# A graph network's prologue rebuilt: blocks ranked ahead of the count, a centred sum of squares, keys and values ahead of the degrees

## The reference, cut to what matters

```python
h = jnp.maximum(_layernorm(x, axis=-1), 0.0)          # input norm, then ReLU
x = x + _L0_gnn_ref(h, edge_index, ...)
# inside, for each of L = 2 layers:
xn = _layernorm(x, ln1_g[l], ln1_b[l])
deg = segment_sum(ones, src); deg = (deg - deg.mean()) / (std(deg, ddof=1) + 1e-6)
pos = xn @ Wpos[l] + bpos[l] + deg[:, None] * Wdeg[l][0] + bdeg[l]
xp = xn + pos
q, k, v = xp @ Wq[l] + bq[l], xp @ Wk[l] + bk[l], xp @ Wv[l] + bv[l]
att = einsum('ehd,ehd->eh', q[dst], k[src]) / scale    # then clip, segment softmax over dst
x = x + (segment_sum(v[src] * alpha, dst) @ Wo[l] + bo[l])
x = x + (gelu(layernorm(x) @ W1[l] + b1[l]) @ W2[l] + b2[l])
```

## Time and profile before

| | us |
|---|---|
| median of 3 runs | 2203.33 (2202.92 to 2208.78) |
| the profiled execution's own time | 2208.83 |
| its span | 2207.1 |
| busy in the span: PE / DVE / ACT / POOL | 1423.0 / 1714.1 / 934.4 / 1578.9 |
| GpSimd's gathers L765, x1612 | 1528.0 busy, 948 ns each |

### The profile page before, as it was taken

The page is one execution under the profiler, slowest core; times in us unless marked ns, Lnnn a source line. Parts: engine busy times, 40 slices in busy tenths (PEclk is TensorE's granted clock), DMA queues, the critical chain, the costliest instruction groups (busy, mean ns, idle before and its releaser), DMA issues.

```text
span 2207.1 us, 32470 instructions
## 1 busy us (share of the span) xinstructions
PE 1423.0 (64%) x8220; PEld 1249.0 (57%) x8220; DVE 1714.1 (78%) x5109; ACT 934.4 (42%) x2172; POOL 1578.9 (72%) x1669
## 2 busy tenths in 40 slices
PE   4765566666767666666666556566575756666666
PEld 3655555555556555655556555555565655555555
DVE  7849878878878878887866777777777778777775
ACT  7424353533535353534453334344353435343343
POOL 6377777777777777777726777777777777777773
PEclk9769888877888887777877878877778778777787
DMA  3355444444444444454424444444444444444441
GB/s 99 100 160 166 141 134 148 130 143 134 136 140 130 149 134 142 131 148 134 137 60 126 135 134 129 134 134 138 134 129 134 138 135 128 135 134 138 125 138 52
DMA packets 123506, 289.30 MB, mean 131 GB/s; under 512 B 31525, under 2 KB 57057, under 8 KB 123329
## 3 DMA queue, kind: packets, MB, share of 16 engines
q0 software_dynamic: 77824, 212.31, 33.5%
q1 hardware_dynamic: 45504, 74.92, 10.4%
HBM read 275.44 MB, written 8.38 MB: 129 GB/s over the span
## 4 chain that ended last, share of the span: by engine, by line
POOL 54%; issue 21%; DVE 8%; PE 8%; DMA 4%; ACT 4%; SPq 1%; DVEq 1%; ACTq 0%; POOLq 0%
POOL kvr L765 52%; DMA kvr<-kv_table,srcidx 4%; PE bank L1005 3%; PE bank L1018 2%; DVE agg L1561 2%; POOL q L726 1%; DVE kvr L1217 1%; ACT apart L1172 1%; DVE prod L1534 1%; ACT onehotT L1176 1%; DVE msg L1552 1%; ACT L1134 1%; PE bank L961 1%; ACT L1181 1%; DVE onehot L1527 1%
## 5 line engine op out<-in xcount | busy, mean ns | idle before, releaser
L765 POOL DMA_INDIRECT kvr<-kv_table,srcidx x1612 | 1528.0, 948 | 560.6 <-issue 480.1
L1005 PE MATMUL bank<-q,onehotT 128*128 x3328 | 610.6, 341 | 717.6 <-DVE prod L1534 455.0
L1005 PEld LDWEIGHTS bank<-q,onehotT 128*128 128x128 f32 x3328 | 518.5, 238 | 821.8 <-issue 821.5
L1018 PE MATMUL bank<-msg,onehot 128*128 128x136 f32 x3328 | 613.9, 344 | 4.1 <-DVE msg L1552 4.0
L1181 ACT ACTIVATE bank<-attc 128x32 f32<-128x32 f32 x404 | 81.2, 201 | 1190.3 <-DVE attc L1547 1189.8
L1018 PEld LDWEIGHTS bank<-msg,onehot 128*128 128x128 f32 x3328 | 575.2, 253 | 5.4 <-DVE msg L1552 5.2
L1534 DVE TENSOR_TENSOR prod<-kvr,bank 128x512 f32<-128x512 f32 x404 | 276.5, 684 | 295.8 <-DMA kvr<-kv_table,srcidx 260.9
L1561 DVE TENSOR_TENSOR agg<-agg,bank 128x136 f32 x1628 | 470.6, 289 | 42.5 <-PE bank L1018 36.5
L1172 ACT ACTIVATE apart<-relT,minus_p 128x512 bf16<-128x512 bf16 x416 | 293.8, 706 | 0.5
L1527 DVE TENSOR_TENSOR onehot<-bank,rel 128x512 f32<-128x512 f32 x416 | 282.6, 682 | 0.4
L1552 DVE TENSOR_TENSOR msg<-kvr,bank 128x512 f32<-128x512 f32 x404 | 274.5, 679 | 7.9 <-ACT bank L1181 7.9
(11 more groups left out here) (205 smaller groups left out, 861.1 us busy)
## 6 DMA issues: line engine op xcount, KB each, us to landing
relT<-rel_table SPq DMA_DIRECT2D x104, 512.0 KB, 4.2
kvr<-kv_table,srcidx POOLq DMA_INDIRECT x1612, 2.8
qkv<-kv_table SPq DMA_DIRECT2D x25, 128.0 KB, 3.4
kv_table<-qkv SPq DMA_DIRECT2D x25, 128.0 KB, 3.1
kv_table<-kvr SPq DMA_DIRECT2D x12, 256.0 KB, 2.1
w<-weights SPq DMA_DIRECT2D x2, 840.0 KB, 7.5
loops<-x_in SPq DMA_DIRECT2D x5, 320.0 KB, 5.4
x<-x_nat SPq DMA_DIRECT2D x25, 64.0 KB, 1.8
```

The lines of the kernel that those rows point to most:

```text
L765: pool.indirect_dma_start(kvr[:, n % RING, j, :], None, kv_table[l], bass.IndirectOffsetOnAxis(ap=srcidx[:, step:step + 1], axis=0)).then_ ...
L1005: mm = pe.matmul(bank[2][:, j * D:(j + 1) * D], onehotT[:, m % OHT, j, :], q[:, bass.ds(ranks[j + h], 1), :].rearrange("p a c -> p (a c)") ...
L1018: mm = pe.matmul(sum_ps(n, k), onehot[:, m % OH, j, :], msg[:, n % 2, j, :], start=(m, j) == of[0], stop=(m, j) == of[-1])
```

## The change

- `rank_blocks` stands ahead of the first count step, `place_steps` between the first and the second.
- The input's squares are taken first, as squares of (first element - x), then the plain sums; DVE corrects the variance by the square of (mean - first element). The squares no longer wait for the mean.
- Layer 1's norm is cut in two halves (12 and 13 blocks), each with its own ReLU, squares, root and normalising pass, interleaved on ACT; DVE's small steps for them stand between the low and the high instruction of a count step.
- The transposes and the first two pairs of keys and values move in between the count steps 10 to 13 on PE. The first four pairs (`KV_EARLY`) are copied out of PSUM with `kv_bias` added before the degrees are known (`keep_early`); `add_degrees` then adds `deg * u` in one instruction per block. For the nine other pairs the bias comes from a three-row matmul on PE (`bias_row`), and the one DVE instruction per block reads PSUM. The order of the pairs is 0, 4, 1, 5, 2, 6, 3, 7, 8 to 12.
- The rows of edge numbers are transposed after the degree sum and before pair 10; layer 2's `u` and fold move behind the queries, the degree's transpose and reordering into the queries, the one-hots of the loop's steps 0 and 1 between query groups 3 and 4.
- SP's 25 copies of the rectified input stand behind the 25 of the queries, ahead of the third `rel_rows`.

```diff
+KV_EARLY = 4
+KV_ORDER = [k for i in range(KV_EARLY) for k in (i, KV_EARLY + i)] + list(range(2 * KV_EARLY, len(KV_PAIRS)))
+HALVES = [(0, 12), (12, BLOCKS)]
...
# SP
-            sp.wait_ge(s_relu, BLOCKS)
-            for b0, nb in NAT:
-                for j, r in enumerate(read_block_ranks(ENG.SP, b0, nb)):
-                    sp.dma_start(x[:, bass.ds(r, 1), :], x_nat[:, b0 + j:b0 + j + 1, :]).then_inc(s_x_ranked, 16)
...
                     sp.dma_start(q[:, bass.ds(r, 1), :], q_nat[:, c % 2, j:j + 1, :]).then_inc(s_q_ranked[c % 2], 16)
+            sp.wait_ge(s_relu, BLOCKS)
+            for b0, nb in NAT:
...
# PE
                 for j in range(nb):
                     o = use(0, i, "kv")[:, j * KV:(j + 1) * KV]
-                    mm = pe.matmul(o, xnT_nat[...], w[0][:, W_QKV + D:W_QKV + 3 * D], start=True, stop=True)
+                    mm = pe.matmul(o, xnT_nat[...], w[0][:, W_QKV + D:W_QKV + 3 * D], start=True, stop=i < KV_EARLY)
+                    if i >= KV_EARLY:
+                        mm = bias_row(o, 0, R_QKV + 1, 2)
...
+                elif k == 10:
+                    turn_nat(0)
+                    turn_nat(1)
+                elif k == 11:
+                    turn_nat(2)
+                    keys_values(0)
+                elif k == 12:
                     turn_bias()
+                    turn_nat(3)
+                    keys_values(1)
+                elif k == 13:
+                    turn_nat(4)
+                    turn_nat(5)
+                    turn_nat(6)
+                elif k == 14:
+                    spread_bias()
...
# ACT
+            rectify(*HALVES[0])
+            square(*HALVES[0])
...
+            first_layer_root(0)
+            rectify(middle, BLOCKS)
+            square(*HALVES[1])
+            first_layer_norm(0)
+            first_layer_root(1)
+            for c in range(3):
+                untranspose_nat(c)
+            act.wait_ge(*read(0, 2, "T"))
+            first_layer_norm(1)
...
# DVE
+            def add_degrees(i):
+                b0, nb = KV_PAIRS[i]
+                k = TURN[0, i, "kv"][0]
+                to = kv_of(b0, nb)
+                if i < KV_EARLY:
+                    dve.wait_ge(*read(0, i, "kv"))
+                else:
+                    dve.wait_ge(*full(0, i, "kv"))
+                for j in range(nb):
+                    of = to[:, j, :] if i < KV_EARLY else bank[k][:, j * KV:(j + 1) * KV]
+                    ins = dve.scalar_tensor_tensor(out=to[:, j, :], in0=u_deg[:, 0, D:3 * D], scalar=deg[:, 0, b0 + j:b0 + j + 1], in1=of, op0=ALU.mult, op1=ALU.add)
```

More of the change, by code:

```diff
@@ L723, in _ @@
             pool.wait_ge(s_tileno, 1)
[L724 to L735, removed]
+            fetch_rows(step_dst, dst_tiles)
+            fetch_rows(step_src, src_tiles)
+            split_bias()
             pool.wait_ge(s_rows, 16 * 2 * SC)
@@ L849, in keys_values @@
                 b0, nb = KV_PAIRS[i]
+                if i == 0:
+                    pe.wait_ge(*read(0, 0, "fold"))
+                pe.wait_ge(*read(0, (b0 + nb - 1) // 4, "T"))
                 claim(0, i, "kv")
@@ L894, in _ @@
+            keys_values(2)
             pe.wait_ge(s_counts, 1)
@@ L1052, in _ @@
                     act.wait_ge(s_x[b // X_BLOCKS], 16)
+                if b == 0:
+                    act.wait_ge(s_digits, 2)
+                act.activation(xn_nat[:, b, :], x_raw[:, b, :], ACT.Square, bias=x_raw[:, b, 0:1], scale=-1.0, accum_out=x_sums[:, 1, b:b + 1]).then_inc(s_squares_in, 1)
+            for b in range(BLOCKS):
                 act.activation(x_nat[:, b, :], x_raw[:, b, :], ACT.Identity, accum_out=x_sums[:, 0, b:b + 1]).then_inc(s_sums_in, 1)
-            act.wait_ge(s_mean_in, 1)
@@ L1055, in _ @@
-            for b in range(BLOCKS):
-                act.activation(x_nat[:, b, :], x_raw[:, b, :], ACT.Square, bias=shift[:, b:b + 1], accum_out=x_sums[:, 1, b:b + 1]).then_inc(s_sums_in, 1)
             root_var(s_var_in, 1, mv[:, :, 1], std[:], s_std)
-            act.wait_ge(s_shift, 1)
-            for b in range(BLOCKS):
-                act.activation(x_nat[:, b, :], x_raw[:, b, :], ACT.Relu, bias=shift[:, b:b + 1], scale=rstd[:, b:b + 1], accum_out=x_sums[:, 0, b:b + 1]).then_inc(s_relu, 1)
@@ L1072, in _ @@
-            root_var(s_var0, 1, mv[:, :, 1], std[:], s_std)
-            act.wait_ge(s_shift, 2)
-            act.wait_ge(s_squares, BLOCKS)
-            for b in range(BLOCKS):
-                act.activation(xn_nat[:, b, :], x_nat[:, b, :], ACT.Identity, bias=shift[:, b:b + 1], scale=rstd[:, b:b + 1]).then_inc(s_xn_nat, 1)
-            act.wait_ge(*full(0, 0, "biasT"))
-            act.copy(bias_parts[:], bank[TURN[0, 0, "biasT"][0]][0:PARTS * L * RC, 0:D]).then_inc(read(0, 0, "biasT")[0], 1)
@@ L1080, in _, with rectify, square @@
-            for c in range(NATS):
+            def rectify(b0, b1):
+                for b in range(b0, b1):
+                    act.activation(x_nat[:, b, :], x_raw[:, b, :], ACT.Relu, bias=shift[:, b:b + 1], scale=rstd[:, b:b + 1], accum_out=x_sums[:, 0, b:b + 1]).then_inc(s_relu, 1)
+            def square(b0, b1):
+                act.wait_ge(s_relu, b1)
+                act.wait_ge(s_squares_in, BLOCKS)
+                for b in range(b0, b1):
+                    act.activation(xn_nat[:, b, :], x_nat[:, b, :], ACT.Square, accum_out=x_sums[:, 1, b:b + 1]).then_inc(s_squares, 1)
@@ new lines, in first_layer_root, with first_layer_norm @@
+            def first_layer_root(h):
+                b0, b1 = HALVES[h]
+                root_var(s_var0, h + 1, mv[:, b0:b1, 1], std[:, b0:b1], s_std)
+            def first_layer_norm(h):
+                b0, b1 = HALVES[h]
+                act.wait_ge(s_shift, h + 2)
+                act.wait_ge(s_squares, b1)
+                for b in range(b0, b1):
+                    act.activation(xn_nat[:, b, :], x_nat[:, b, :], ACT.Identity, bias=shift[:, b:b + 1], scale=rstd[:, b:b + 1]).then_inc(s_xn_nat, 1)
@@ L1187, in _ @@
             edge_spread(1)
+            for l in range(1, L):
+                keep_degree(l)
             for l in range(L):
@@ L1348, in _ @@
+            dve.wait_ge(*read(0, 0, "wide"))
+            keep_early(0)
+            keep_early(1)
             dve.wait_ge(s_hist_mm, HSTEPS)
```

302 lines of the change are left out of this document (171 added, 131 removed).

## The result

The changed kernel takes 2200.52 us in the median (2197.87 to 2206.04, 12 runs), the kernel before 2205.26 on the same chip (2202.92 to 2209.64, 12 runs). The ratio is 0.9979, 95% interval [0.997, 0.9988]: 4.7 us faster, 2.6 to 6.6 by the interval. Forecast were 11.9 us. The profiled execution took 2200.12 us, its span 2198.4. It is 8.7 us shorter than the profiled execution before (2208.83), which was one of the slower ones of its kernel: the traces, one execution each, show more of the gain than the medians do.

A forecast was written before the change was run, and what follows sets the result against it. The loop runs at GpSimd's gather pace, so the first gather's start and the messages' lead decide. The smaller of 13.9 and 9.7 + 2.2, 11.9 us, off the 2203.33 median gives about 2191.5 us; range 2186 to 2206.

The forecast's parts named there:

- The rule: Loop start: the kernel gains the smaller of G and A + 2.2, forecast 11.9 us.
- ring: Messages ahead of the loop's gathers: least slack of the first steps 2.2 us, at the 45th gather, needing step 3's message.
- G: How much earlier GpSimd's first gather starts: 13.9 us, at 97.0 instead of 110.9.
- A: How much earlier the loop's first product on DVE comes: 9.7 us, at 128.3 instead of 137.96.
- I take nothing, with 0 and 3 us as bounds: SP: third rel_rows queued behind the 25 copies of x leaves some 12 us after the first product, just in time.
- some 4 us: Time for the third rel_rows load to land, wanted by ACT about 16 us after the first product.
- The second term: Prologue to GpSimd's first gather: count steps, then pairs bound by PE, put it at 97.0.
- the count ends after 76: Sign that the forecast is wrong; DVE's count was laid out to end at 72.5, against 81.2 before.
- DVE's row: DVE up to the count's end: 6.4 + 2.5 us of waits gone, 1 new, about 1 for the start.
- Rival 1: PE's clock falls in the pairs of keys and values: gain 2.6, time 2200.7; chance 0.2.
- Rival 2: GpSimd is kept out for several count steps, more than once: 2208.5 with three such waits, 2220 with four; chance 0.09.
- Rival 3: Queries hold the loop back, first product only 3 us earlier: gain 5.2, time 2198; chance 0.09.

The follow-up runs named there:

- experiment 3: Changed kernel with SP's 25 copies of x back in their old place, ahead of the count's end: 2196.04 us, ratio 0.9954 to the kernel before.
- experiment 4: Changed kernel with only the third rel_rows load issued ahead of the 25 copies of x: 2197.36 us, ratio 0.9957 to the kernel before.
- its repetition: Changed kernel, unchanged, measured and profiled once more: 2200.53 us, ratio 0.9974 to the kernel before.
- Experiment 8: experiment 3's kernel with three of GpSimd's four operations on 128x896 given to ACT: 2194.94 us, ratio 0.9948 to the kernel before.
- experiment 6: Changed kernel, third rel_rows load behind 12 of 25 copies, or behind 25 plus 12 more; first on a slow chip, rerun: 2198.82 and 2207.64 us.

## Why the prediction was wrong

**The rule held, within some 2 us.** First gather and ring decide. The prediction's rule, the smaller of G and A + 2.2, gives 8.6 us for experiment 3 with its own first gather and first product (102.3 and 130.4), 7.7 for experiment 4 (103.2 and 131.8). Measured are 10.1 (7.5 to 13.0) and 9.5 (6.0 to 12.8).

**The step that failed is SP's: "I take nothing, with 0 and 3 us as bounds".** Putting the 25 copies of x ahead of the third `rel_rows` cost 0.0021 of the ratio, 4.6 us: the mean of after and its repetition (0.99765) against that of experiments 3 and 4 (0.99555). By the widths of the four intervals this is an estimate of 2 to 7 us. Two things in the step were wrong.

The first is the time to land. The forecast had the load leave 12 us behind the first product, land in "some 4 us" and be wanted at 16. It left at 11.4, was wanted at 14.8 (146.16 - 3.10) and had landed at 17.9. So landing took 6.5 us. The trace of the kernel before shows it for this one load, in a window around its issue (size in KB, median us from issue to landing):

```profile
relT<-rel_table SPq DMA_DIRECT2D x1, 512.0 KB, 6.4
```

The second is what the delay falls on. The forecast charged it to step 4's message, which leads its gather by 3 us. But step 3's message stands behind step 4's product on DVE, and it has the least lead of all, 2.2 us, of which 0.3 pass between a message's end and the gather that it frees (156.15 and 156.43). It came 2.0 us later against the first product; with 1.9 us of lead, and 0.1 by which the first gather gained more than the first product (9.8 and 9.7), that makes the 0.2 us in the trace. So the chain of waits is shown, but this execution lost 0.2 us by it, not 4.6.

**The second term off is the first gather.** 101.1 instead of 97.0. The count ends 3.7 us late, PE starts the first pair with bias 2.2 late (81.61 instead of 79.4), and 8.5 pairs of 1.70 instead of 1.5 are 1.7 more. The prediction named "the count ends after 76" as a sign against itself, and it ended at 76.2. By the rule min(G, A + 2.2) this turns 11.9 into min(9.8, 9.7 + 2.2) = 9.8. So 11.9 - 2.1 for the gather - 4.6 for SP's load = 5.2 us, and the mean of both runs of after gives 0.00235 x 2205 = 5.2. That the two agree to a tenth is luck: the 4.6 is a difference of the same ratios, and each of them is uncertain by 2 us or more.

**DVE's row.** The waits of 6.4 and 2.5 us went, as forecast. In their place came 0.9 more than laid out at `position_bias`, and 2.45 + 0.73 between 45.93 and 54.35, where GpSimd's operations on 128x896 lie, 4.1 in all, against a count that ends 3.7 late. Experiment 8 shows that GpSimd's operations cause the second part. The page "SBUF — State Buffer" of the Trainium skill, section "SBUF: two separate sides", says that a DVE instruction with two inputs in SBUF and a GpSimd instruction that reads SBUF contend for a lock, which goes to whoever starts first for the whole instruction. I had weighed only that GpSimd comes late; this trace agrees for the other direction as well, DVE being late by 2.45 us.

**Rivals.** Rival 1 (the clock falls in the pairs): false, 1.00 from 79 to 98 us. Rival 2 (GpSimd is kept out over several count steps): false, no fetch took over 2.5 us and GpSimd was done with the last of this work by 54.3. Rival 3 (the queries hold the loop back): false, the first product came 9.7 us earlier as forecast, though its time (2198) is near the measured one. PE's queries ran at 2.4 GHz for the greater part (0.93 from 98 to 115), where I had priced 1.2 GHz; SP's copies, 19.8 us as before, set the first product all the same.

**What stays open.** Where the 4.6 us of the medians go. The profiled executions show 0.2 and 0.5 us of them as a late 45th gather in the kernel after, and where the load left behind 12 copies they show none, while its time is 3 us above that of the load first. Nor do they show the rest elsewhere: from the first gather to the end of the span are 2097.3 and 2093.9 us in the two profiles of after, 2094.3 and 2098.4 in those of experiments 3 and 4, and much of that spread is the wait for layer 2's table (42.3 to 48.2 us over the profiles, those on the slow chip of experiment 6 left aside). Either the lateness differs from one execution to the next and the profile caught mild ones, or a part of it is the copies' traffic after all. The intervals, 2 to 3.5 us to each side, don't tell these apart. Beyond the threshold the price is clear, in trace and time: 8 us later cost 10 us at the gather and 6 to 7 in the time.

## What to carry to other kernels

Where a ring hides latency, its slack is one account: add up everything that draws on it (a late first product, a late load, a slower queue) before pricing any of them at nothing. Follow a late item through each engine's order to the first thing that stands behind it: here it was the message of the step before, not its own. Take the time to land from the very load in question. When copies are moved behind something in an in-order DMA queue, look at what stood behind their new place and by when its data are wanted, and issue the wanted load first. An operation on GpSimd that is "hidden" may still be paid by DVE where both run, so place it beside DVE's waits or give it to an idle ScalarE.

## What the runs showed of the hardware

- A bf16 matmul of three rows between f32 matmuls of 128x256 costs PE 0.40 us a block at 2.4 GHz (1.70 against 0.90 a pair), more than its own row of 0.28.
- Operations of GpSimd on 128x896 lengthen DVE's two-input bf16 instructions beside them by 2.45 us over three (7.60 against 5.15), and the stretch follows the operation when it is moved (6.22 against 4.74). GpSimd pays too: the first of these conversions took 0.97 us in the kernel before, at 64.11, where DVE did no count step, and 2.30 in the kernel after, at 44.04.
- A GpSimd fetch (an indirect DMA) can be held over many DVE instructions: the one of 13.08 us beside DVE's eight came in both profiles of the kernel before, where a free one takes 0.94.
- The third load of 512 KB took 6.4 us to land in the kernel before and 9.4 behind 37 copies, while the median of all 104 such loads is 4.2 in both.
- The queries' pattern of matmul and three-row bias ran at a granted clock of 0.50 for 20 us in the kernel before and at 0.93 from 98 to 115 us in the kernel after. Experiment 8's kernel does the same work there, has PE just as full, and ran at 0.61:

```profile
98.00:115.00 17.00, 17.00 (x66) 11.13 (x64) 8.62 (x27) 0.85 (x2) 10.41 (x11) 0.61 0.56 157
```

  What decides it, these runs don't show.
- One chip ran the same kernel 29% slower (2838 us), with PE's granted clock at 0.69 and GpSimd waiting for messages. The clock need not be the cause: DVE stood idle for 720 us ahead of its additions to `agg` (L1658), instead of 46 for the same kernel on the other chip, and for most of it the profile names nothing in this kernel that ended the wait. What bounds a kernel can change with the chip; the kernel before, run in the same job, is what shows it.
